# A Strassen-like FFN kernel: both tiles' y made in one stay of TensorE instead of two

## The reference, cut to what matters

```python
y = einsum('bct,bcd->bdt', x, weights[itok])          # 64 samples, 64x64 matrix chosen per sample
x_flat = y.reshape(-1, 1024)
logits = x_flat @ gate_w.T + expert_bias              # 4 experts
top1 = argmax(logits)
base = x_flat @ W_up.T                                # 1024 x 1024
z = x_flat @ lora_A                                   # rank 8 per expert
out = x + base + (z of the chosen expert) @ lora_B
```

## Time and profile before

| what | value |
|---|---|
| median of 3 runs | 406.23 us (405.65 to 406.31) |
| profiled execution, its own time | 405.92 us |
| its span in the trace | 404.1 us |
| PE busy | 398.5 us, 99% of the span |
| PE weight loads | 358.3 us, 89% |
| DVE busy | 300.8 us, 74% |
| ACT busy | 110.3 us, 27% |
| POOL busy | 129.1 us, 32% |
| granted TensorE clock | full in all 40 slices |

### The profile page before, as it was taken

How to read it: one execution, slowest core, us unless ns; L and a number is a source line. 1 busy time by engine, 2 the same in 40 slices (tenths; PEclk the granted TensorE clock), 3 DMA queues, 4 the chain that set the end, 5 groups by cost and what they waited for, 6 DMA issues and landing times.

```text
span 404.1 us, 9748 instructions
## 1 busy us (share of the span) xinstructions
PE 398.5 (99%) x3451; PEld 358.3 (89%) x3451; DVE 300.8 (74%) x719; ACT 110.3 (27%) x226; POOL 129.1 (32%) x121
## 2 busy tenths in 40 slices
PE   8899999999999999999999999999999999999997
PEld 8899988989888898988979798898988889898996
DVE  3899668889876859676696766867677766967775
ACT  5896211323114031312213130130311203131310
POOL 1687302529031350505205080221605043050710
PEclk9999999999999999999999999999999999999999
DMA  7910330503214123413125032150332221250102
GB/s 255 350 62 2 122 101 28 190 27 113 87 66 145 53 87 105 133 55 113 50 78 187 28 109 68 49 177 26 110 104 93 95 79 58 104 182 27 54 32 99
DMA packets 20993, 39.39 MB, mean 97 GB/s; under 512 B 7494, under 2 KB 7750, under 8 KB 20970
## 3 DMA queue, kind: packets, MB, share of 16 engines
q1 hardware_dynamic: 17600, 27.40, 18.9%
q10 hardware_dynamic: 3370, 11.69, 9.3%
HBM read 22.30 MB, written 16.78 MB: 97 GB/s over the span
## 4 chain that ended last, share of the span: by engine, by line
PE 96%; DMA 1%; SPq 1%; ACT 1%; issue 0%; DVE 0%
PE bank_y L878 23%; PE bank_x L878 22%; PE bank_b L878 11%; PE bank_c L929 10%; PE y_ps L791 7%; PE bank_c L1083 5%; PE bank_b L1083 4%; PE bank_x L856 2%; DMA cond_pair<-in_L_cond_weights_dram 1%; PE bank_c L878 1%; PE bank_b L884 1%; PE bank_x L884 1%; PE bank_y L884 1%; PE bank_c L884 1%; PE bank_y L856 1%; PE y_ps L1157 1%
## 5 line engine op out<-in xcount | busy, mean ns | idle before, releaser
L878 PE MATMUL bank_y<-w_s,hl_s 128*128 128x292 f32 (+1 forms) x384 | 51.5, 290 | 0.0
L878 PEld LDWEIGHTS bank_y<-w_s,hl_s 128*128 128x128 f32 x384 | 49.2, 188 | 2.5 <-issue 2.5
L878 PE MATMUL bank_x<-w_a,hl_a 128*128 128x256 f32 (+1 forms) x384 | 50.8, 288 | 0.0
L878 PEld LDWEIGHTS bank_x<-w_a,hl_a 128*128 128x128 f32 x384 | 49.5, 188 | 0.4
L878 PE MATMUL bank_y<-w_a,hl_a 128*128 128x292 f32 x360 | 47.7, 288 | 0.0
L878 PE MATMUL bank_b<-w_s,hl_s 128*128 128x512 f32 x192 | 47.7, 397 | 0.0
L878 PEld LDWEIGHTS bank_y<-w_a,hl_a 128*128 128x128 f32 x360 | 46.6, 188 | 0.3
L307 POOL TENSOR_TENSOR s_sum<-a 128x512 f32<-128x512 f32 x9 | 11.6, 1287 | 105.5 <-DVE a L1405 102.4
L878 PE MATMUL bank_x<-w_s,hl_s 128*128 128x292 f32 x336 | 44.6, 289 | 0.0
L929 PE MATMUL bank_c<-w_s,hl_s 128*128 128x512 f32 x168 | 44.4, 410 | 0.0
L878 PEld LDWEIGHTS bank_x<-w_s,hl_s 128*128 128x128 f32 x336 | 43.1, 188 | 0.1
(11 more groups left out here) (193 smaller groups left out, 619.1 us busy)
## 6 DMA issues: line engine op xcount, KB each, us to landing
out_dram<-x_sb SPq DMA_DIRECT2D x63, 256.0 KB, 2.0
x_sb<-in_x_dram ACTq DMA_DIRECT2D x22, 512.0 KB, 3.6
x_sb<-in_x_dram SPq DMA_DIRECT2D x10, 512.0 KB, 3.4
w_raw<-in_L_ffn_W_up_dram SPq DMA_DIRECT2D x8, 512.0 KB, 5.8
cond_pair<-in_L_cond_weights_dram SPq DMA_DIRECT2D x64, 16.0 KB, 2.7
out_dram<-x_sb SPq DMA_DIRECT2D x2, 128.0 KB, 1.9
router_sb<-in_L_ffn_lora_A_dram ACTq DMA_DIRECT2D x1, 128.0 KB
lora_b_sb<-in_L_ffn_lora_B_dram SPq DMA_DIRECT2D x1, 128.0 KB, 5.2
```

The source lines that it names most:

```text
L878: mm = pe.matmul(dst, hl[op][:, a, k, :], w[:, b, k, cols], start=(fresh and k == 0 and a + b == 0), stop=(k == KH - 1 and a == 1), skip_g ...
```

## The change

In every block the y of both tiles is made in one stay. It stands behind s3's product, in odd blocks behind the last quarter q4. The first tile's y goes into the pair's banks (`bank_x` or `bank_y`), which are free once c11 is drained; the second tile's y goes to `y_ps` as before. DVE's list is put in a new order: it scores and routes first, turns the first tile (from the pair's banks), drains s3, makes a11's low part, turns the second tile, makes a12's low part, and only then drains the last three output quarters. In even blocks these are now in the order c22, c21, c12 (before: c12, c21, c22), in block 1 and the odd ones c21, c12, c22 (before: c12, c21, c22).

```diff
@@ tensor
-            def wait_y_inputs(q, par, t):
-                pe.wait_ge(x_loaded[2 * par + t], 8 * (q - par) + 16)
-                pe.wait_ge(pair_loaded[2 * par + t], 16 * (q - par) + 32)
-                pe.wait_ge(y_summed, 4 * q + 2 * t)
+            def wait_y_inputs(q, par):
+                for t in range(2):
+                    pe.wait_ge(x_loaded[2 * par + t], 8 * (q - par) + 16)
+                    pe.wait_ge(pair_loaded[2 * par + t], 16 * (q - par) + 32)
+                pe.wait_ge(y_summed, 4 * q)
+                pe.wait_ge(c11_out, q)
+            def make_both_y(q, par, pair):
+                make_y(q, par, 0, pair)
+                make_y(q, par, 1, y_ps)
             def third_product(q, pair):
                     if k == KH - 1:
+                        pe.wait_ge(y_summed, 4 * q + 6)
                         turn_second_z(q, pair)
@@ even (one: the same)
-                multiply("s2", q, chain, False, lambda: wait_y_inputs(q + 1, 1, 0))
-                make_y(q + 1, 1, 0)
+                multiply("s2", q, chain, False)
...
-                multiply("s3", q, chain, False, lambda: wait_y_inputs(q + 1, 1, 1))
-                make_y(q + 1, 1, 1)
+                multiply("s3", q, chain, False, lambda: wait_y_inputs(q + 1, 1))
+                make_both_y(q + 1, 1, pair)
                 third_product(q, pair)
@@ odd
-                wait_y_inputs(q + 1, 0, 0)
                 delta11_of(q, pair)
-                make_y(q + 1, 0, 0)
                 pe.wait_ge(u2_out, q + 1)
                 multiply("s3", q, chain, False)
                 pe.wait_ge(quarter_out, quarters(g, 7))
-                wait_y_inputs(q + 1, 0, 1)
+                wait_y_inputs(q + 1, 0)
                 q4(g)
-                make_y(q + 1, 0, 1)
+                make_both_y(q + 1, 0, pair)
@@ scalar, first even block only: round_a11 now stands behind round_fine(6) and round_fine(4)
```

More of the change, by code:

```diff
@@ L744, in even @@
                 move_z(q, 0, 0, bank_c[:, 0, :])
-                round_a11(q + 1, True)
                 if isinstance(g, int) and g == 0:
@@ L750, in even @@
                     round_fine(4)
+                round_a11(q + 1, True)
                 round_a12(q + 1, True)
@@ L778, in _, with make_y @@
         def _(pe):
-            def wait_y_inputs(q, par, t):
-                pe.wait_ge(x_loaded[2 * par + t], 8 * (q - par) + 16)
-                pe.wait_ge(pair_loaded[2 * par + t], 16 * (q - par) + 32)
-                pe.wait_ge(y_summed, 4 * q + 2 * t)
-            def make_y(q, par, t):
+            def wait_y_inputs(q, par):
[4 more added lines that the diff above has]
+                pe.wait_ge(c11_out, q)
+            def make_y(q, par, t, bank):
                 for d in range(2):
@@ L790, in make_y @@
                             at = b * D + d * STRIP
-                            mm = pe.matmul(y_ps[j * STRIP:(j + 1) * STRIP, b, d * QUARTER:(d + 1) * QUARTER],
+                            mm = pe.matmul(bank[j * STRIP:(j + 1) * STRIP, b, d * QUARTER:(d + 1) * QUARTER],
                                            cond_pair[rows, 2 * par + t, at:at + STRIP],
@@ L919, in turn_second_z @@
             def turn_second_z(q, pair):
-                pe.wait_ge(c11_out, q + 1)
                 turn_z(pair[:, 1, 0:P], q, 1)
@@ L1024, in _ @@
             multiply("s1", 0, bank_b, True)
+            pe.wait_ge(c11_out, 1)
             turn_second_z(0, bank_y)
@@ L1043, in one @@
                 pe.wait_ge(p1_out, q + 1)
-                multiply("s2", q, chain, False, lambda: wait_y_inputs(q + 1, 0, 0))
-                make_y(q + 1, 0, 0)
+                multiply("s2", q, chain, False)
                 pe.wait_ge(p4_out, q)
@@ L1051, in one @@
                 pe.wait_ge(u2_out, q + 1)
-                multiply("s3", q, chain, False, lambda: wait_y_inputs(q + 1, 0, 1))
-                make_y(q + 1, 0, 1)
+                multiply("s3", q, chain, False, lambda: wait_y_inputs(q + 1, 0))
+                make_both_y(q + 1, 0, pair)
                 third_product(q, pair)
@@ L1173, in close @@
                 multiply("s1", q, bank_b, True)
+                pe.wait_ge(c11_out, q + 1)
                 turn_second_z(q, pair)
@@ L1316, in after_delta11, with score_p7, add_p7, after_p7 @@
                 add_pair(chains[1 - par], par, 0, 0).then_inc(c11_out, 1)
-            def after_p7(q, par):
+            def score_p7(q, par):
                 dve.wait_ge(product_done["s3"], q + 1)
                 score(chains[par], bias_sb)
+            def add_p7(q, par):
                 add_pair(chains[par], par, 1, 1).then_inc(u3_out, 1)
+            def after_p7(q, par):
+                score_p7(q, par)
+                add_p7(q, par)
             def after_delta12(q, par):
@@ L1396, in _, with turn_y @@
             low_operand(dve, "a22", a22, 1)
-            def turn_y(q, t, h, to):
+            def turn_y(q, t, h, to, bank):
                 if to is a12:
@@ L1406, in turn_y, with turn_first_tile, turn_second_tile @@
                         to[:, :].rearrange("p (k b d n) -> p b d k n", k=KH, b=2, d=2)[:, b, :, :, :],
-                        y_ps[:, b, :].rearrange("p (d h k n) -> p h d k n", d=2, h=2, k=KH)[:, h, :, :, :])
+                        bank[:, b, :].rearrange("p (d h k n) -> p h d k n", d=2, h=2, k=KH)[:, h, :, :, :])
                 turned.then_inc(y_summed, 1)
+            def turn_first_tile(q, bank):
+                turn_y(q, 0, 0, a11, bank)
+                turn_y(q, 0, 1, a12, bank)
+            def turn_second_tile(q, last):
+                turn_y(q, 1, 0, a21, y_ps)
+                turn_y(q, 1, 1, last, y_ps)
             def rebuild(k, n):
@@ L1427, in one @@
                 after_p6(q, 1)
-                turn_y(q + 1, 0, 0, a11)
-                turn_y(q + 1, 0, 1, a12)
                 dve.wait_ge(lora_stage[1], HIGH)
@@ L1435, in one @@
                 after_p5(q, 1)
-                low_operand(dve, "a11", a11, q + 1)
                 after_delta11(q, 1)
@@ L1439, in one @@
                 rebuild(1, 1)
-                low_operand(dve, "a12", a12, q + 1)
[L1441 to L1445, removed]
+                score_p7(q, 1)
+                route(q, 1, 1)
+                turn_first_tile(q + 1, chains[0])
+                add_p7(q, 1)
+                low_operand(dve, "a11", a11, q + 1)
+                turn_second_tile(q + 1, a22_even)
+                low_operand(dve, "a12", a12, q + 1)
                 dve.wait_ge(p4_out, q)
                 after_delta21(q, 1)
+                after_delta12(q, 1)
                 after_delta22(q, 1)
@@ L1481, in even @@
                 low_even_a22(g)
+                score_p7(q, 0)
+                route(q, 0, 1)
+                turn_first_tile(q + 1, chains[1])
+                add_p7(q, 0)
+                low_operand(dve, "a11", a11, q + 1)
+                turn_second_tile(q + 1, a22)
                 low_operand(dve, "a12", a12, q + 1)
[L1483 to L1486, removed]
+                after_delta22(q, 0)
+                after_delta21(q, 0)
                 after_delta12(q, 0)
-                after_delta21(q, 0)
-                after_delta22(q, 0)
                 if isinstance(g, int) and g == 0:
@@ L1548, in odd @@
                 after_delta11(q, 1)
-                turn_y(q + 1, 0, 0, a11)
-                turn_y(q + 1, 0, 1, a12)
+                score_p7(q, 1)
+                route(q, 1, 1)
+                drain(4, g, bank_c, 3, 0, 0)
+                add_p7(q, 1)
+                turn_first_tile(q + 1, chains[0])
                 low_operand(dve, "a11", a11, q + 1)
-                after_p7(q, 1)
-                drain(4, g, bank_c, 3, 0, 0)
-                route(q, 1, 1)
+                turn_second_tile(q + 1, a22_even)
                 low_operand(dve, "a12", a12, q + 1)
-                turn_y(q + 1, 1, 0, a21)
-                turn_y(q + 1, 1, 1, a22_even)
-                after_delta12(q, 1)
                 dve.wait_ge(quarter_out, quarters(g, 4))
                 after_delta21(q, 1)
+                after_delta12(q, 1)
                 after_delta22(q, 1)
```

## The result

| | median | range | runs |
|---|---|---|---|
| before, in the same series | 405.76 us | 405.26 to 406.31 | 5 |
| changed kernel | 414.47 us | 413.40 to 415.09 | 5 |

The ratio is 1.0213, 95% interval 1.0198 to 1.0228: the changed kernel is 8.7 us slower. Its profiled span is 413.1 us against 404.1.

A forecast was written before the change was run, and what follows sets the result against it. PE, busy 99% of the span, was taken as the bound: 4.2 us saved by joining against 13.0 lost to waits, net 8.8 later, 414.7 from the profiled 405.92, stated as 415.0; range 409.5 to 418.5.

The forecast's parts named there:

- the likeliest case: Whole kernel: c12's lateness goes through load_x and the POOL exclusion bites; 412.5 to 418.5 us, chance 0.60.
- Joining saves: PE's y stays: one joined stay saves 0.26 us in block 1 and even blocks, 0.35 in odd ones, together 4.2.
- The rival that the second bank costs an entry: Joined stay on PE: PE drains between the two tiles, so joining saves nothing, 4.2 less saved, 419 us; chance 0.06.
- c12's lateness and load_x: DVE and ACT: c12 starts 2.14 us later in even tails, 1.20 in odd; load_x and ACT's queue behind it equally late.
- A: Time mark the prediction counts from: the start of a block's a11 product on PE.
- POOL and low q5: Odd blocks: low q5 on DVE comes up behind POOL's L320 and waits, stalling q5 1.30 us in five blocks, 6.5.
- A walk of ten steps: Timing walk to low q5 in odd blocks: ten DVE steps and one DMA, an error of 0.3 us called well possible.
- the other outcome: Odd blocks: low q5 slips in ahead of L320, stall only 0.4 to 0.5 us, total 410.8; chance 0.20.
- s2 in even blocks: Even blocks 6 to 14: s2's low part is 1.20 us late against slack 0.89, stalling PE 0.31 each, 1.5 together.
- s3 in odd blocks: Six odd blocks: without the stay ahead of it, s3 waits for its low part, 0.22 us each, 1.3 together.
- Blocks 2 and 3: POOL and DVE also form fine weights there and block each other more: 1.3 us lost each, 2.6 together.
- this term: Block 4: its load_x already has 0.8 us less slack, so s2 loses 0.31 + 0.8 = 1.1.

The follow-up runs named there:

- experiment 2: Changed kernel, its drain order kept, with load_x moved behind round_s2 in ACT's queue: 403.54 us, ratio 0.9953 to the kernel before.
- experiment 7: Changed kernel with load_x behind round_s2 and, in odd blocks, s3's low part made ahead of s4's on DVE: 401.96 us, ratio 0.9904.
- experiment 3: Changed kernel, but in odd blocks POOL waits for q5's low part before starting L320: 410.75 us, ratio 1.0130.
- experiment 1: Changed kernel with c12 drained first again in both tails (c12, c21, c22): 406.50 us, ratio 1.0029.
- experiment 8: Changed kernel with c12 first in both tails, and POOL held in even blocks until s2's low part is made: 404.28 us, ratio 0.9971.
- experiment 5: Changed kernel with c12 first in the tails of even blocks alone, odd tails keeping c21, c12, c22: 406.54 us, ratio 1.0023.
- experiment 4: Kernel before with only the changed kernel's order of the last drains, stays left separate: 411.86 us, ratio 1.0164.
- experiment 6: Kernel before with load_x moved behind round_s2 in ACT's queue and nothing else: 406.16 us, ratio 1.0002.

## Why the prediction was right, point by point

**The time.** 415.0 was forecast, 414.47 measured, in the likeliest case's range of 412.5 to 418.5 and on its side of 405.76. The number is not a sum of large errors that cancel: block by block the forecast and the measured change are 5.9 and 6.0 for the five odd blocks, 1.0 and 1.0 for block 2, 1.2 and 0.9 for block 3, 0.8 and 1.0 for block 4, 0.3 and 0.6 for the later even blocks, -0.3 and -0.3 for block 1.

**Joining saves.** Forecast 0.17 for the stay itself, measured 2.04 - 1.88 = 0.16. With the entries, even blocks were to save 0.26; where nothing else waits (experiment 2) they take 20.92 against 21.15, so 0.23. That these are so close is in part luck. The stay, s2's slot (3.11 to 3.02) and the slot of the z behind it (0.08 to 0.03, which the sum left out) save 0.30; and in blocks 6 to 12 a11's own slot is 3.08 to 3.13 instead of 3.02, its second matmul starting 0.1 late, which takes some back. That 0.1 is also in blocks 6, 8 and 12 of the changed kernel; its cause was not looked for. Odd blocks were to save 0.35 and in experiment 7, free of waits, save 26.45 - 26.07 = 0.38. The rival that the second bank costs an entry is out.

**c12's lateness and load_x.** Forecast c12 at A + 1.87 and A + 0.85, load_x 3.0 behind. Measured 143.39 - 141.62 = A + 1.77 and 170.19 - 169.34 = A + 0.85, load_x 3.04 and 3.03 behind. That load_x is the carrier was an inference from two equal distances; experiment 2 shows it.

**POOL and low q5.** Forecast low q5 at A + 6.28 and a start of q5 at A + 8.77, a stall of 1.30. Measured A + 6.22, A + 8.66 and 1.19. The forecast had 0.27 between L320's start and low q5; it was 0.30, with L320 at A + 5.92 (forecast A + 6.0), so both came 0.1 early together. A walk of ten steps that had to be right to 0.3 was right to 0.1; the prediction itself gave 0.20 to the other outcome. Experiment 3 shows that the meeting with POOL is worth 5 x 0.60 = 3.0 us of the time of odd blocks; the rest of the 3.7 by which the time fell goes with block 4, which in that execution did not have its late load.

**s2 in even blocks.** Forecast 0.31, measured 0.31 in block 6 and 0.35 on the mean of blocks 6 to 14. The prediction did not walk POOL in even blocks at all. L315 ended 0.01 before low s2 came up (A + 5.50 and A + 5.51 in block 6), which was luck; experiments 1 and 8 show that without c12's lateness low s2 would have met L315: the two causes cover each other, and the 0.31 could not have been won by the order of drains alone.

**s3 in odd blocks.** Forecast 0.22, measured 0.48 - 0.24 = 0.24 on the deltas' slot and another 0.07 on s3's own (experiment 7).

**Sizes that were off.** Blocks 2 and 3 were costed at 1.3 each without a walk. Net of the savings block 2 came to 1.0 and block 3 to 0.9, where 1.0 and 1.2 had been forecast. The reason given there, fine weights on POOL and DVE, is at most a small part: with load_x moved (experiment 2) block 2 takes 21.3 as in the kernel before and block 3 26.7 against 26.5, so their loss too went mostly through load_x. Left out altogether: the first group behind a wait is slower, q5's slot being 0.81 instead of 0.72 and s2's 3.10 instead of 3.02, about 0.1 for each wait. An even block was forecast 0.05 longer (0.31 - 0.26) and came out 0.13 longer: 0.35 for s2's start and 0.08 for its slot, less the 0.30 saved.

**What stays open.** Block 4, the first that runs in the loop, had its load_x at A + 4.9 in the changed kernel and at A + 3.8 in experiment 5, where c12 stands at the same place in the odd tail. c12's store, which this load_x waits for, is issued 0.7 after the start of the drain in both, but takes 3.1 us to land in the changed kernel and 2.0 in experiment 5; in the kernel before it took 3.0 in block 4 and 2.0 in block 6. I had taken this delay of the first loop pass as fixed and costed 0.8 for it. Of the ten profiled executions only those of the kernel before and of the changed kernel have it, so that this term came out was luck. No run tells why the store takes longer there.

## What to carry to other kernels

Look for the first wait in every in-order queue. A load that nothing needs soon costs nothing as long as its wait ends early, and costs the whole queue once the work it waits for moves: here a drain moved by two microseconds within DVE's list stalled PE through a store, a load's wait, ACT, POOL and a second drain. Moving the load behind the urgent work made the same change a gain, and a change of order should be tried with each of its parts alone before it is judged: here the joined stays were worth -2.0 us with load_x out of the way (experiment 2) and -3.8 with s3's low part moved as well (experiment 7), and the drains' order +6.3 alone (experiment 4) and +6.8 to +8.0 beside the joined stays (experiments 5 and 1).

## What the runs showed that I had not expected

- Making an engine wait can save time. Held back by a semaphore, POOL's L320 let low q5 through in 0.43 us instead of 1.27, and the five odd blocks together took 3.0 us less (experiment 3).
- The order of three drains of 0.68 us each, with no other change, cost 6.3 us (experiment 4), and c12 moved by 1.67 rather than by two drains' 1.20, because the one now in front waits for PE's last instruction.
- Experiments 1, 5 and 8 spread over 2.4 to 4.0 us between executions (10 to 12 of each), where experiment 2 spread over 0.4 (4 executions). In the first three load_x stands at the head of ACT's queue with little slack left, so small variations of a store's landing could reach PE. But the kernel before, with its full slack, itself spread over 2.3 us in 29 executions beside experiments 5 to 8, and the stretch ahead of block 1 alone differs by 1.0 us between the profiled executions. So the cause of the spread is not shown.
